# Softmax reciprocals spread over the keys by DMA through DRAM instead of by matmuls, with four score slots, in a cross-attention kernel

## The chip, the cores and the metric

The kernel runs on one core of one Trainium2 chip. The metric is the device time of one execution in microseconds (us). The kernel before takes 1735.91 us, the median of three runs (1733.51 to 1736.13).

## The reference

Cross-attention of 16 batches, 1024 query tokens each, with 64 context keys, 16 heads of 64 columns and a model width of 512; then a residual and a layer norm. Cut to what matters:

```python
qh = (q @ Wq + bq).reshape(Bn, Tq, H, DK)
kh = (k @ Wk + bk).reshape(Bn, Tk, H, DK)
vh = (v @ Wv + bv).reshape(Bn, Tk, H, DK)
attn = jnp.einsum('bqhd,bkhd->hbqk', qh, kh)
attn = attn * mask[None]
attn = attn - jnp.max(attn)
attn = jnp.exp(attn) * mask[None]
attn = attn / (jnp.sum(attn, axis=-1, keepdims=True) + 1e-15)
out = jnp.einsum('hbqk,bkhd->bqhd', attn, vh).reshape(Bn, Tq, H * DK)
out = out @ Wo + bo
x = out + residual
mu = jnp.mean(x, axis=-1, keepdims=True)
var = jnp.mean((x - mu) ** 2, axis=-1, keepdims=True)
return (x - mu) / jnp.sqrt(var + 1e-05) * gamma + beta
```

The maximum is taken over all scores of all batches, so no exponential can be formed before the last score is known. The sum that divides is one number for each token and head, and it divides that head's 64 keys.

## The kernel before

The kernel is written engine by engine: SP issues every DMA (one queue), and PE, ACT, DVE and POOL each have their own list of instructions, in the order in which the code lists them, with semaphores between them. Nothing reorders the work. There are two phases.

**Scores phase** (`scores_phase`, up to 917 us). Query and key weights are folded into one matrix for each batch, values and output weights into another, U. A *unit* is one batch's half of the tokens (512 of them); there are 32 units, four to a group (`UNITS`), eight groups. A unit's scores are a tile of 128 partitions (two heads of 64 keys) x 8 head pairs x 512 tokens, float32, 2 MB. Units 2 to 31 of the output phase's order are written to DRAM (`scores_d`); the last two that are made stay in SBUF in the two slots of `s32` and become units 0 and 1.

**Output phase** (`output_phase`, from 917 us on). In unit n:

- PE makes the unit's output: four token blocks t of 128, for each the eight head pairs p, and for each of these three float16 matmuls (L79 to L81, `add_product`): 96 matmuls with 512 columns. In between it does work for later units. `sums(n + 2)` (L792, before block t = 1, pair p = 7) adds the exponentials of unit n + 2 over each head's keys: 16 matmuls, as float32. `spread(n + 1, p)` (L804, eight places in the unit, table `spread_at`) copies the reciprocals of unit n + 1 from the few partitions where they stand to all 64 keys of each head, into a PSUM bank `ps_bc`. PE has float32 only in pieces here, so the reciprocal is first cut into three bfloat16 parts (`r_hi`, `r_mid`, rest).
- ACT rounds the scaled exponentials to float16 (`round_p`, L870), forms the exponentials of unit n + 2 in two halves in place (`exps`, L856), puts the bias into the output banks (`fill`, L875), cuts the reciprocals (`r_first`, `r_second`, L860, L864) and applies the norm (`norm`, L880).
- DVE multiplies exponentials and spread reciprocals (`scale_p`, L960, SBUF times PSUM into PSUM), takes the rounding rest (`split_p`, L964), inverts the sums (`invert`, L941 and L943), makes the second and third part of the reciprocals (L947, L954), adds the residual and takes the layer norm's statistics (`residual`, L975 to L980) and its shift (`shift_of`, L986).
- POOL computes 1 / sqrt(var + eps) (L1061, L1064) and applies gamma and beta (L1071, L1073).
- SP loads scores of unit n + 2 into the slot that unit n leaves (L722), the input x of unit n + 2 (L730), U of a batch in every second unit (L734), and stores the output of unit n - 1 (L740).

ACT's last two calls in a unit are `fill(n + 1, 3)` and `norm(n, 3)`. `norm(n, 3)` has to wait for PE's last block of unit n, then for DVE's statistics, POOL's `rstd` and DVE's shift, so it runs when PE is some us into unit n + 1. ACT's calls for unit n + 1 stand behind it.

Of the kernel before, what the change touches and what calls it, by code (L numbers as in the profile page):

```python
# [13 lines left out]
P = 128  # L14
# [8 lines left out]
TT = 512  # L23
# [18 lines left out]
COPIES = 3  # L42


def build(nc, xT, x, ctxT, maskT, wk, wqT, wv, wo, bk, bq, bv, bo, gamma, beta,
          sel_sum_d, sel_bc_d, part_d, out):

    scores_d = nc.dram_tensor("scores", (NU - UB, P, NP * TT), F32, kind="Internal").ap()
    u_d = nc.dram_tensor("u_halves", (B, P, NP * 2 * D), F16, kind="Internal").ap()

    with ExitStack() as ctx:
        def sb(name, shape, dt=F32, scope=ctx):
# [4 lines left out]
        sel_sum, sel_bc = sb("sel_sum", [P, NP // 2, 32]), sb("sel_bc", [P, NP, 2, P], BF16)  # L57
# [3 lines left out]
        scores_phase(nc, xT, ctxT, maskT, wk, wqT, wv, wo, bk, bq, bv, sel_bc_d, scores_d, u_d,  # L61
                     s32, sel_bc, score_max, least)
        output_phase(nc, x, scores_d, u_d, bo, gamma, beta, sel_sum_d, part_d, out,
                     s32, sel_sum, sel_bc, score_max, least, key_max, neg_max)
# [59 lines left out]
def scores_phase(nc, xT, ctxT, maskT, wk, wqT, wv, wo, bk, bq, bv, sel_bc_d, scores_d, u_d,  # L124
                 s32, sel_bc, score_max, least):

    with ExitStack() as ctx:
# [96 lines left out]
        def _(sp):  # L224
# [6 lines left out]
            def load_sel():  # L231
                sp.wait_ge(w_lo_done, 16)
                for i in range(2):
                    sp.dma_start(w32[:, i, :], sel_bc_d[i]).then_inc(w_loaded(16 + i)[0], 16)

# [43 lines left out]
            def group(g, first, last):  # L279
# [8 lines left out]
                for u in range(UNITS):  # L288
# [6 lines left out]
                    if first and u == 2:  # L295
                        load_sel()
# [115 lines left out]
        def _(act):  # L412
# [59 lines left out]
            def copy_sel(i):  # L472
                act.wait_ge(*w_loaded(16 + i))
                act.activation(sel_bc[:, 4 * i:4 * i + 4, :, :].rearrange("r p t k -> r (p t k)"),
                               w32[:, i, :], ACT.Copy)

            def scores_out(g, u, first, last):
# [11 lines left out]
                for p in range(NP):  # L489
# [16 lines left out]
                    if first and u == 2 and p in (3, 5):  # L506
                        copy_sel(p // 4)
# [149 lines left out]
def output_phase(nc, x, scores_d, u_d, bo, gamma, beta, sel_sum_d, part_d, out,  # L657
                 s32, sel_sum, sel_bc, score_max, least, key_max, neg_max):
# [3 lines left out]
    with ExitStack() as ctx:  # L662
# [13 lines left out]
        part = sb("part", [P, 2])  # L676
# [8 lines left out]
        r32, rest = ps_sum[:, HT:2 * HT], ps_sum[:, 0:HT]  # L685

# [448 lines left out]
```

## Time and profile before

| | |
|---|---|
| median of three runs | 1735.91 us (1733.51 to 1736.13) |
| profiled execution, its own time | 1737.56 us |
| its span, first to last instruction | 1735.8 us |
| PE busy | 1676.3 us, 97% |
| DVE / ACT / POOL busy | 1153.6 / 938.8 / 419.0 us |
| DMA | 315 MB, 181 GB/s over the span |
| scores phase / junction / output phase | 0 to 917 / 917 to 950 / 950 to 1736 us |

The span is one execution taken by the profiler; its own time lies 1.76 us over the span and 1.65 us over the median. Busy PE time counts overlapping matmuls once, so 97% says that PE rarely waits, not that it is at its peak. A matmul of 512 columns is shown with 380 ns, but the next one starts 216 ns after it.

### The profile page before, as it was taken

How to read it: one execution, taken by the hardware profiler on the slowest of the kernel's cores; microseconds unless marked ns; L12 is line 12 of the kernel's file. 1: busy time of each engine (PE TensorE's matmuls, PEld its weight loads, DVE VectorE, ACT ScalarE, POOL GpSimd, SP SyncE). 2: the span in 40 equal slices, each digit the busy share in tenths (PEclk: the TensorE clock that was granted, in tenths of full speed). 3: DMA queues.
4: the chain of work that ended last, by engine and by line, in shares of the span. 5: the costliest groups of instructions: out<-in, count | busy, mean ns of one | idle time of the engine just before them, and what ended most of it. 6: DMA issues, size and time to landing. Idle time of an engine off the chain costs nothing. (4 is left out here: it accounts for less than half of the span.)

```text
span 1735.8 us, 31156 instructions
## 1 busy us (share of the span) xinstructions
PE 1676.3 (97%) x11011; PEld 858.7 (49%) x11012; DVE 1153.6 (66%) x2346; ACT 938.8 (54%) x1413; POOL 419.0 (24%) x519
## 2 busy tenths in 40 slices
PE   4989999999999999999995999999999999999997
PEld 4545556455564655646542444444444444444443
DVE  7756555655556654565544877787787878787774
ACT  7745555455555555455544556555555656555542
POOL 0000000000000000000000455555555555555556
PEclk8999999999999999999996999999999999999999
DMA  6464344443544526445235356555654556555621
GB/s 231 146 230 141 146 182 163 178 167 121 205 159 161 187 91 235 137 168 196 74 146 209 139 230 242 217 206 205 242 209 186 194 233 242 217 201 210 242 104 67
DMA packets 81469, 315.01 MB, mean 181 GB/s; under 512 B 5392, under 2 KB 9616, under 8 KB 71696
## 3 DMA queue, kind: packets, MB, share of 16 engines
q1 hardware_dynamic: 81424, 314.41, 49.4%
q8 instruction: 28, 0.46, 0.1%
q14 instruction: 17, 0.14, 0.0%
HBM read 184.37 MB, written 130.02 MB: 181 GB/s over the span
## 5 line engine op out<-in xcount | busy, mean ns | idle before, releaser
L70 PE MATMUL ps_s<-x_hi,g_hi 128*128 128x512 f16 x1024 | 388.4, 379 | 7.0 <-ACT s L494 7.0
L79 PE MATMUL ps_o<-u,p_hi 128*128 128x512 f16 x1024 | 389.3, 380 | 0.0
L80 PE MATMUL ps_o<-u,p_hi 128*128 128x512 f16 x1024 | 388.9, 380 | 0.0
L81 PE MATMUL ps_o<-u,p_lo 128*128 128x512 f16 x1024 | 388.6, 380 | 0.0
L71 PE MATMUL ps_s<-x_lo,g_hi 128*128 128x512 f16 x1024 | 388.1, 379 | 0.0
L72 PE MATMUL ps_s<-x_hi,g_lo 128*128 128x512 f16 x1024 | 388.1, 379 | 0.0
L494 ACT ACTIVATE s<-ps_s,c_bias 128x512 f32<-128x512 f32 x256 | 175.8, 687 | 334.1 <-PE ps_s L72 330.2
L603 DVE TENSOR_TENSOR score_max<-score_max,tile_max 128x1 f32<-128x1 f32 x257 | 40.8, 159 | 339.2 <-ACT s L494 336.9
L870 ACT ACTIVATE p_hi<-ps_bc 128x512 f16<-128x512 f32 x256 | 149.4, 593 | 178.5 <-DVE ps_bc L960 176.6
L1051 POOL PARTITION_ALL_REDUCE key_max<-score_max x1 | 0.4, 377 | 922.8 <-issue 922.8
L1071 POOL TENSOR_TENSOR y<-y,gamma_b 128x512 f32<-128x512 f32 x128 | 162.7, 1271 | 192.7 <-ACT y L880 192.7
L960 DVE TENSOR_TENSOR ps_bc<-s,ps_bc 128x512 f32<-128x512 f32 x256 | 174.3, 692 | 19.4 <-PE ps_bc L804 15.8
L964 DVE TENSOR_TENSOR p_lo<-ps_bc,p_hi 128x512 f16<-128x512 f32 x256 | 175.4, 685 | 4.4 <-ACT p_hi L870 3.7
L613 DVE CUSTOM_DVE_ANT_0 s<-s,mask_add 128x512 f32<-128x512 f32 x256 | 176.6, 690 | 0.0
L880 ACT ACTIVATE y<-y,shift,rstd 128x512 f32<-128x512 f32 x128 | 104.0, 813 | 131.2 <-DVE shift L986 131.2
L1073 POOL TENSOR_TENSOR y<-y,beta_b 128x512 f32<-128x512 f32 x128 | 162.5, 1270 | 10.0
L70 PEld LDWEIGHTS ps_s<-x_hi,g_hi 128*128 128x128 f16 x1024 | 100.1, 98 | 130.8 <-issue 10.3
L81 PEld LDWEIGHTS ps_o<-u,p_lo 128*128 128x128 f16 x1024 | 100.3, 98 | 121.5 <-issue 1.1
L72 PEld LDWEIGHTS ps_s<-x_hi,g_lo 128*128 128x128 f16 x1024 | 100.2, 98 | 120.9
L71 PEld LDWEIGHTS ps_s<-x_lo,g_hi 128*128 128x128 f16 x1024 | 100.2, 98 | 112.0
L79 PEld LDWEIGHTS ps_o<-u,p_hi 128*128 128x128 f16 x1024 | 100.3, 98 | 104.4 <-issue 14.0
L80 PEld LDWEIGHTS ps_o<-u,p_hi 128*128 128x128 f16 x1024 | 100.4, 98 | 91.1 <-issue 0.6
(85 smaller groups left out, 2423.0 us busy)
## 6 DMA issues: line engine op xcount, KB each, us to landing
scores<-s SPq DMA_DIRECT2D x30, 2048.0 KB, 7.6
s<-scores SPq DMA_DIRECT2D x30, 2048.0 KB, 7.7
x<-xT_in SPq DMA_DIRECT2D x32, 1024.0 KB, 9.7
u_halves<-u_out SPq DMA_DIRECT2D x64, 512.0 KB, 2.9
u<-u_halves SPq DMA_DIRECT2D x16, 2048.0 KB, 11.8
y<-x_in SPq DMA_DIRECT2D x32, 1024.0 KB, 10.0
out<-y SPq DMA_DIRECT2D x31, 1024.0 KB, 4.3
mask<-maskT_in SPq DMA_DIRECT2D x32, 256.0 KB, 10.3
```

The source lines that it names most:

```text
L70: pe.matmul(out, lhs_hi, rhs_hi, start=first, stop=False)
L71: pe.matmul(out, lhs_hi, rhs_lo, start=False, stop=False)
L72: return pe.matmul(out, lhs_lo, rhs_hi, start=False, stop=last)
L79: pe.matmul(out, lhs_hi, rhs_hi, start=False, stop=False, skip_group_check=True)
L80: pe.matmul(out, lhs_hi, rhs_lo, start=False, stop=False, skip_group_check=True)
L81: return pe.matmul(out, lhs_lo, rhs_hi, start=False, stop=False, skip_group_check=True)
L494: act.activation(s32[:, u % 2, p, :], ps_s[p % SBANKS][:, :], ACT.Identity, bias=c_bias[:, k:k + 1], scale=1 / (G_SCALE * X_SCALE)).then_i ...
L613: dve.tensor_tensor_reduce(s32[:, u % 2, p, :], s32[:, u % 2, p, :], mask_add[:, j, t0:t0 + TT], 1.0, MASKED, ALU.add, ALU.max, tile_max[: ...
L960: dve.tensor_tensor(spread, s32[:, s, p, :], spread, ALU.mult).then_inc(p_scaled, 1)
L964: dve.tensor_tensor(p_lo[:, s, p, :], ps_bc[p % RBANKS][:, :], p_hi[:, s, p, :], ALU.subtract)\
L1071: pool.tensor_tensor(y, y, gamma_b[:, :], ALU.mult).then_inc(scaled, 1)
L1073: pool.tensor_tensor(y, y, beta_b[:, :], ALU.add).then_inc(shifted, 1)
```

## The change

The reciprocals are no longer multiplied out by PE. DVE writes them into SBUF (`r32`, [128, 2, 256], already scaled), SP stores them to a small DRAM tensor `r_d` with four DMAs of 8 partitions x 256 numbers (`store_r`), waits until all four have landed, and reads them back with four DMAs, each into 64 partitions x 4 pairs x 512 tokens, in which every one of a head's 64 partitions gets the same row (`spread_r`, 512 KB a DMA, 2 MB a unit). The three bfloat16 parts, the selector matrix `sel_bc` and its load are gone. `scale_p` multiplies two SBUF tiles and writes PSUM. There are four score slots (two in `s32`, two in `s_more`), and SP loads scores three units ahead instead of two. ACT's two `exps` move to the start of a unit's list, PE's `sums` from (1, 7) to (1, 0), DVE's `invert` from behind `split(3)` to behind the first `residual`.

The diff, cut to its core:

```diff
+    r_d = nc.dram_tensor("reciprocals", (2, NP, 2, TT), F32, kind="Internal").ap()
...
-        den = sb("den", [P, HT])
-        r_hi, r_mid, r_all = sb("r_hi", [P, HT], BF16), sb("r_mid", [P, HT], BF16), sb("r_all", [P, 2, HT], BF16)
+        s_more = sb("s_more", [P, 2, NP, TT])
+        den, r32 = sb("den", [P, 2, HT]), sb("r32", [P, 2, HT])
+        r_bc = sb("r_bc", [P, 2, NP, TT])
...
-        spread_at = {(0, 2): 0, (0, 5): 1, (1, 0): 2, (1, 3): 3, (1, 6): 4, (2, 1): 5, (2, 4): 6, (2, 7): 7}
-        sums_at = (1, 7)
+        sums_at = (1, 0)
+
+        def scores_of(u):
+
+            return (s32 if u % UNITS < 2 else s_more)[:, u % 2, :, :]
...
             def load_scores(n, u):
-                sp.wait_ge(p_scaled, (n - 1) * NP)
+                if not isinstance(n, int) or n >= UNITS:
+                    sp.wait_ge(p_scaled, (n - UNITS + 1) * NP)
...
+            def store_r(n, s):
+
+                sp.wait_ge(r_done, n + 1)
+                for q in range(4):
+                    th, a = q // 2, q % 2
+                    sp.dma_start(r_d[s, 4 * a:4 * a + 4, :, th * HT:(th + 1) * HT].rearrange("p h t -> (p h) t"),
+                                 r32[32 * q:32 * q + NP, s, :]).then_inc(r_stored, 16)
+
+            def spread_r(n, s):
+
+                sp.wait_ge(r_stored, 64 * n + 64)
+                for k in range(2):
+                    for h in range(2):
+                        row = r_d[s, 4 * k:4 * k + 4, h:h + 1, :].rearrange("p a t -> a p t")
+                        sp.dma_start(r_bc[rows_of(h), s, 4 * k:4 * k + 4, :], row.to_broadcast([NK, 4, TT]))\
+                          .then_inc(bc_in[s][k], 16)
...
             sp.dma_start(sel_sum[:, :, :], sel_sum_d).then_inc(sum_in, 16)
-            sp.dma_start(part[:, :], part_d).then_inc(sum_in, 16)
+            load_scores(2, 2)
+            load_scores(3, 3)
             load_u(0, B - 1)
...
+            for n in range(2):
+                store_r(n, n)
+                spread_r(n, n)
...
+                    n = g * UNITS + u
+                    if not (first and u == 0):
+                        store_y(g, u - 1)
                     if not (last and u >= UNITS - 2):
-                        load_scores(g * UNITS + u + 2, u)
+                        store_r(n + 2, u % 2)
+                        spread_r(n + 2, u % 2)
+                    if not (first and u == 0) and not (last and u >= UNITS - 3):
+                        load_scores(n + 3, u + 3)
+                    if not (last and u >= UNITS - 2):
                         load_x(g, u + 2)
...
+            pe.wait_ge(u_in[0], 16)
             for o in ps_o:
-                mm = pe.matmul(o[:, :], sel_bc[:, 0, 0, :], sel_bc[:, 0:2, :, :].rearrange("r p t k -> r (p t k)"),
-                               start=True, stop=True)
+                mm = pe.matmul(o[:, :], u2[:, 0, 0, 0, 0:P], u2[:, 0, 0, 0, :], start=True, stop=True)
             mm.then_inc(o_written, 1)
...
-                    halves(0, 1)
                     if more2:
-                        exps(n + 2, u, 0)
-                    halves(2)
+                        exps(n + 2, u + 2, 0)
+                    halves(0)
                     if more2:
-                        exps(n + 2, u, 1)
-                    halves(3)
+                        exps(n + 2, u + 2, 1)
+                    halves(1, 2, 3)
...
+            def scale_p(n, u, p):
+                s = u % 2
+                if p % 4 == 0:
+                    dve.wait_ge(bc_in[s][p // 4], 16 * n - 16 * s + 32)
...
+                dve.tensor_tensor(ps_p[p % RBANKS][:, :], scores_of(u)[:, p, :], r_bc[:, s, p, :], ALU.mult)\
+                   .then_inc(p_scaled, 1)
```

How the instructions stand on SP, first before, in unit 2 of group 0 (out names the tile written; `y` is the residual and output tile):

```order
L722 DMA s<-scores 128x4096 [waits p_scaled]
L730 DMA y<-x_in 128x4x512 [waits y_stored0]
L734 DMA u<-u_halves 128x8192 [waits o_summed]
L740 DMA out<-y 128x4x512 [waits shifted]
L722 DMA s<-scores 128x4096 [waits p_scaled]
```

and in the changed kernel, for the same unit:

```order
L744 DMA out<-y 128x4x512 [waits shifted]
L718 DMA reciprocals<-r 8x256 [waits r_done]
L718 DMA reciprocals<-r 8x256 x3
L727 DMA r_bc<-reciprocals 64x4x512 [waits r_stored]
L727 DMA r_bc<-reciprocals 64x4x512 x3
L709 DMA s<-scores 128x4096 [waits p_scaled]
L734 DMA y<-x_in 128x4x512 [waits y_stored0]
L738 DMA u<-u_halves 128x8192 [waits o_summed]
```

The scores' load, which stood first, now stands behind eight new DMAs and the two waits in front of them.

ACT's list at the change of units, first before (the last norm of a unit, then the next unit, in the last group):

```order
L880 ACTIVATE y<-y,shift,rstd 128x512 [waits shift_done]
L870 ACTIVATE p_hi<-ps_bc 128x512 [waits p_scaled,o_summed]
L870 ACTIVATE p_hi<-ps_bc 128x512 [waits p_scaled]
L856 ACTIVATE s<-s,neg_max 128x2x1024 [waits s_in1]
L870 ACTIVATE p_hi<-ps_bc 128x512 [waits p_scaled]
L856 ACTIVATE s<-s,neg_max 128x2x1024 [waits s_in1]
```

and in the changed kernel:

```order
L871 ACTIVATE y<-y,shift,rstd 128x512 [waits shift_done]
L855 ACTIVATE s_more<-s_more,neg_max 128x2x1024 [waits s_in3]
L861 ACTIVATE p_hi<-ps_p 128x512 [waits p_scaled,o_summed]
L855 ACTIVATE s_more<-s_more,neg_max 128x2x1024 [waits s_in3]
```

The exponentials stand two roundings earlier, but still behind the previous unit's last norm.

PE's list around the sums in the last group (`ps_sum` holds the sums), first before, in the second token block:

```order
L804 MATMUL ps_bc<-r_all,sel_bc 128x256 [waits p_lo_done]
L804 MATMUL ps_bc<-r_all,sel_bc 128x256
L79 MATMUL ps_o<-u,p_hi 128x512
L80 MATMUL ps_o<-u,p_hi 128x512
L81 MATMUL ps_o<-u,p_lo 128x512
L792 MATMUL ps_sum<-s,sel_sum 32x256 [waits exp_done,r_all_done]
L792 MATMUL ps_sum<-s,sel_sum 32x256 x7
L792 MATMUL ps_sum<-s,sel_sum 32x256 [waits exp_done]
```

and in the changed kernel, where the first token block ends:

```order
L78 MATMUL ps_o<-u,p_hi 128x512 [waits p_lo_done]
L79 MATMUL ps_o<-u,p_hi 128x512
L80 MATMUL ps_o<-u,p_lo 128x512
L806 MATMUL ps_sum<-s_more,sel_sum 32x256 [waits exp_done,den_done,bo_filled]
L806 MATMUL ps_sum<-s_more,sel_sum 32x256 x7
L806 MATMUL ps_sum<-s_more,sel_sum 32x256 [waits exp_done]
L806 MATMUL ps_sum<-s_more,sel_sum 32x256 x7
L78 MATMUL ps_o<-u,p_hi 128x512
```

Before, 15 triples of the unit and five of its eight `ps_bc` pairs stood ahead of the sums. Now eight triples do, and the `ps_bc` pairs are gone.

## Rows read from the trace of the kernel before

**Rows 1.** Windows of the output phase: us, busy of PE, PEld, DVE, ACT, POOL, PEclk, DMA, GB/s.

```profile
950.50:1683.50 733.00, 733.00 (x4313) 353.96 (x4312) 582.07 (x1076) 411.75 (x598) 386.48 (x474) 1.00 0.55 210
...
1268.11:1292.54 24.43, 24.43 (x145) 11.81 (x144) 19.45 (x36) 13.72 (x20) 13.06 (x16) 1.00 0.45 170
```

**Rows 2.** Chain that ended last, in order of time: start us, us, what.

```profile
1254.64 1.86 PE ps_sum L792 x32
1279.07 1.86 PE ps_sum L792 x32
```

**Rows 3.** Timeline of PE, unit 13: start us, us, engine, line, operation.

```profile
1268.11 0.38 PE L79 MATMUL ps_o<-u,p_hi 128*128 128x512 f16 x1
...
1278.04 0.38 PE L804 MATMUL ps_bc<-r_all,sel_bc 128*128 128x256 bf16 x2
...
1279.00 1.93 PE L792 MATMUL ps_sum<-s,sel_sum 128*32 128x256 f32 x32
1280.87 0.39 PE L79 MATMUL ps_o<-u,p_hi 128*128 128x512 f16 x1
...
1292.54 0.38 PE L79 MATMUL ps_o<-u,p_hi 128*128 128x512 f16 x1
```

**Rows 4.** Timeline of ACT, from a unit's last norm through the next unit's exponentials.

```profile
1271.80 0.81 ACT L880 ACTIVATE y<-y,shift,rstd 128x512 f32<-128x512 f32 x1 [2.17 <-DVE shift L986]
...
1273.50 2.00 ACT L856 ACTIVATE s<-s,neg_max 128x2048 f32<-128x2048 f32 x1
1275.39 0.59 ACT L870 ACTIVATE p_hi<-ps_bc 128x512 f16<-128x512 f32 x1
1275.87 2.00 ACT L856 ACTIVATE s<-s,neg_max 128x2048 f32<-128x2048 f32 x1
```

**Rows 5.** Timeline of DVE: an inversion; a unit's last shift and the next unit's first scales.

```profile
1256.57 0.42 DVE L941 TENSOR_SCALAR den<-ps_sum 128x256 f32<-128x256 f32 x1 [1.25 <-PE ps_sum L792]
1257.03 1.76 DVE L943 RECIPROCAL ps_sum<-den 128x256 f32<-128x256 f32 x1
...
1271.55 0.21 DVE L986 TENSOR_SCALAR shift<-mean_var,rstd 128x1 f32<-128x1 f32 x1 [1.57 <-POOL rstd L1064]
1271.68 1.29 DVE L960 TENSOR_TENSOR ps_bc<-s,ps_bc 128x512 f32<-128x512 f32 x2
```

**Rows 6.** Timeline of POOL across the same change of units.

```profile
1269.48 1.27 POOL L1073 TENSOR_TENSOR y<-y,beta_b 128x512 f32<-128x512 f32 x1
...
1272.69 1.27 POOL L1071 TENSOR_TENSOR y<-y,gamma_b 128x512 f32<-128x512 f32 x1 [1.18 <-ACT y L880]
```

**Rows 7.** Timeline of SP, the store of the previous unit's output.

```profile
1275.59 0.40 SPq L740 DMA_DIRECT2D out<-y  x1
```

**Rows 8.** DMA issues: operation, count, KB each, median us from issue to landing.

```profile
s<-scores SPq DMA_DIRECT2D x30, 2048.0 KB, 7.7
...
y<-x_in SPq DMA_DIRECT2D x32, 1024.0 KB, 10.0
...
out<-y SPq DMA_DIRECT2D x4, 256.0 KB, 2.0
```

**Rows 9.** DMA rates in 40 slices of 104 to 114 us; the low ones are mask loads.

```profile
GB/s 369 377 369 377 377 385 385 369 426 426 434 295 213 254 213 246 221 197 172 172 172 172 262 385 434 418 410 426 393 377 361 442 377 442 393 426 442 393 442 393
```

**Rows 10.** DMA rates in 40 slices of 924 to 934 us; gamma, beta, bo repeated over partitions.

```profile
GB/s 328 459 524 393 352 238 262 361 352 402 385 279 123 131 115 147 74 172 197 238 295 254 262 311 369 401 385 410 434 410 410 401 401 393 418 401 418 401 352 328
```

**Rows 11.** PE in windows around the junction: us, PE busy, PEclk, DMA share, GB/s.

```profile
925.96:929.74 3.78, 3.72 (x32) 0.53 1.01 230
...
947.60:950.08 2.48, 0.01 (x2) 0.99 0.95 405
950.08:953.04 2.96, 2.96 (x9) 0.50 1.04 381
```

**Rows 12.** Timeline: the first exponentials, and DVE's first work after PE's last matmul.

```profile
923.81 3.89 ACT L856 ACTIVATE s<-s,neg_max 128x2048 f32<-128x2048 f32 x2 [7.59 <-DVE neg_max L1031]
...
1726.92 0.69 DVE L975 SCALAR_TENSOR_TENSOR y<-ps_o,y 128x512 f32<-128x512 f32 x1 [2.36 <-PE ps_o L81]
```

More of the change, by code:

```diff
@@ L684, in output_phase @@
         ps_sum = bank("ps_sum")
-        r32, rest = ps_sum[:, HT:2 * HT], ps_sum[:, 0:HT]
-        ps_bc = [bank(f"ps_bc{i}") for i in range(RBANKS)]
+        ps_p = [bank(f"ps_p{i}") for i in range(RBANKS)]
         ps_o = [bank(f"ps_o{i}") for i in range(OBANKS)]
@@ L792, in sums @@
                         mm = pe.matmul(ps_sum[32 * q:32 * q + 32, 0:HT], sel_sum[:, i, :],
-                                       s32[:, s, p, th * HT:(th + 1) * HT],
+                                       scores_of(u)[:, p, th * HT:(th + 1) * HT],
                                        start=(i == 0), stop=(i == 3), skip_group_check=True)
                 mm.then_inc(e_summed, 1)
-            def spread(n, s, p):
-                if p == 0:
-                    pe.wait_ge(r_all_done, n + 1)
-                pe.wait_ge(p_lo_done, n * NP + (p + 1 if p >= RBANKS else (2, 3, 1)[p]))
-                for th in range(2):
-                    mm = pe.matmul(ps_bc[p % RBANKS][:, th * HT:(th + 1) * HT], sel_bc[:, p, th, :], r_all[:, s, :],
-                                   start=True, stop=True)
-                mm.then_inc(r_spread, 1)
             def unit(g, u, last):
                 n, s, b = g * UNITS + u, u % 2, u // UB
-                more, more2 = not (last and u == UNITS - 1), not (last and u >= UNITS - 2)
+                more2 = not (last and u >= UNITS - 2)
                 if u % UB == 0:
@@ L817, in unit @@
                     for p in range(NP):
[L818 to L819 removed]
                         if more2 and (t, p) == sums_at:
[L821 removed]
+                            sums(n + 2, u + 2)
                         if t == 0:
[L823 removed]
+                            pe.wait_ge(p_lo_done, n * NP + p + 1)
                         cols = slice(t * P, (t + 1) * P)
@@ L918, in _ @@
             exps(1, 1, 1)
-            r_first(0)
-            r_second(0)
             act.wait_ge(affine_in, 48)
@@ L926, in _ @@
                     fill(0, p // 2)
-            r_first(1)
-            r_second(1)
             with act.Fori(0, NG - 1) as g:
@@ L992, in group @@
                     more, more2 = not (last and u == UNITS - 1), not (last and u >= UNITS - 2)
-                    scale = lambda p: scale_p(n, s, p) if more else None
+                    scale = lambda p: scale_p(n, u + 1, p) if more else None
                     split = lambda p: split_p(n, s, p) if more else None
@@ L1122 @@
         "bo": a["bo"], "gamma": a["gamma"], "beta": a["beta"],
[L1123 removed]
+        "sel_sum": sel_sum,
     }
```

141 lines of the change are left out of this document (40 added, 101 removed).

## The prediction

> **What bounds the kernel now.** I read the windows first: from 950.5 to 1683.5 us PE is busy for all 733 us at full clock (level 2.4 GHz), while DVE has 19.45 us of work in a unit, ACT 13.7, POOL 13.1, and the DMA engines are half used [rows 1]. So the output phase is PE's own time. The chain of waits says the same: it runs through PE only, and the sums of one unit start 24.43 us after those of the unit before [rows 2]. A unit (here 13, from 1268.11 to 1292.54) is thus 24.43 us: 96 matmuls 0.216 us apart, 20.75; sums 1.87 (1279.00 to 1280.87); and what is left, 1.81, is the eight pairs of `ps_bc` matmuls [rows 3]. The change takes away those 1.81 us, 31 times, at most 56 us. The rest of this text asks what the unit waits for instead.
>
> **What hides at no cost.** `r_first`, `r_second`, the second and third part on DVE and the selector's load go; they lay beside PE's work. The scores phase is otherwise as it was.
>
> **Sums and exponentials.** Call U the start of a unit on PE. PE now wants the sums of unit n + 2 after eight triples, at U + 5.2. The exponentials stand behind the previous unit's last norm on ACT. That norm starts at U + 3.7 (1271.80), after DVE's shift (1271.55), which waited for POOL, which first finished the affine begun at 1269.48 [rows 4 to 6]. The change moves nothing of this. So the first exponential starts at E = U + 4.4 at the earliest. The first half ends 2.0 us later, one rounding lies between, and the second half ends at E + 4.4 (1273.50 to 1277.87) [rows 4]. The first half of the sums can end at E + 3.0, the second at E + 5.4, which is U + 9.8. PE wanted to be through at U + 7.1 and stalls 2.7 us. With 24 triples behind it (15.55) a unit is at least 25.4 us. If POOL were free sooner, E would be U + 3.7 and the unit 24.7. Either way, what the spreads gave back is gone here alone. Before, this stall was not there, because PE asked at U + 10.9 for halves that ended at U + 9.8.
>
> **The ring of waits through the DMA queue.** SP issues in the order: output of n - 1, four stores of the reciprocals of n + 2, wait until landed, four spreads, scores of n + 3, x, U. The scores of n + 3 are wanted by the exponentials at the start of the next unit, E'. So E' hangs on E:
>
> - exponentials, both halves: 4.4 [rows 4];
> - second half of the sums: 0.95 at full clock; 1.9 after a stall, since after 2.5 us without work PE's clock is at 0.50 (1.2 GHz) for the next 3 us, and the sums at 926 took 3.78 us instead of 1.86 [rows 2, 11]. Taken: 1.9;
> - DVE adds and inverts: 2.2 (1256.57 to 1258.79) and 0.1 to get there [rows 5]. `r_done` at E + 8.6;
> - four stores. An issue holds SP 0.4 us [rows 7], and a small transfer, 256 KB, lands 2.0 us after it [rows 8]: 0.1 + 1.2 + 2.0 = 3.3. At E + 11.9. SP stands still for that, with the scores, x and U of the unit queued behind;
> - spreads: 0.9 from issue to first data (an estimate: 7.7 us for 2 MB less 6.0 of transfer at 350 GB/s and 0.8 of landing) [rows 8], then 2 MB in 64-partition DMAs that repeat one row over the partitions. No row has this. Nearest in width are the mask loads, 64 partitions each: eleven slices between 172 and 295 GB/s, mean 212, with 370 to 430 on both sides [rows 9]; 2.10 MB at 212 is 9.9 us. Nearest in source are the three loads that repeat one row over 128 partitions: 0.79 MB pass in about 3.5 us, 230 GB/s, six slices of it at 127 [rows 10]. From below: 400 GB/s as the neighbours have, 5.2 us. From above: 127, 16.5 us. I take 10.5, by the masks with a little for the source;
> - scores, 2.10 MB at the 400 GB/s of a filled queue [rows 9]: 5.2, landing 0.8 [rows 8].
>
> Sum 4.4 + 1.9 + 2.3 + 3.3 + 0.9 + 10.5 + 5.2 + 0.8 = 29.3; 29.4 with rounding. This is more than the 25.4 that PE and ACT need, so the ring sets the period, and PE stands still some 5 us in each unit. After the stall up to 3 us of matmuls run at half clock [rows 11], 1.5 us lost, but they are covered: U' = E + 6.3 + 1.5 + 15.55 = E + 23.4, and with 4.4 that is E + 27.8, below 29.4. x and U (2.6 and 5.2 us) of an even unit end at about E' + 7, the store of the output (issued at U' + 7.5 [rows 7], 2.6 us) behind them at E' + 9.6, before the reciprocals' stores should land at E' + 11.9; so they don't lengthen it.
>
> The Trainium skill, SBUF — State Buffer, section "Door 1: The DMA port swizzle", says that 64 partitions in a row reach only 8 of 16 ports, half of 435 GB/s. By that the spreads would take 9.6 us instead of 10.5 and the forecast would be 24 us lower; the masks' mean of 212 agrees with it.
>
> DVE loses 0.96 us of work in a unit. `scale_p` reads two SBUF tiles; I keep its 0.6 us start to start (1271.68, 1.29 for two) [rows 5].
>
> **Junction.** Before, unit 1 starts at 975.0 (1268.11 less 12 x 24.43). Now SP first issues 4 MB of scores, U, three repeated rows and 2 MB of x from 918 us on. PE waits for U before its first sums: 919 + 3 x 5.2 = 935. `r_done` of unit 0 is at about 941 (before 932: exponentials from 923.81 [rows 12], sums and inversion). Its stores land at 946 behind x, half its spread at 953. DVE and ACT need 1.2 us for each pair, the second four wait for the other half at 958.4: PE has the eighth pair at 963.5. The spread of unit 1 is issued only after the first (SP waits for its stores), its first half lands at 965.6. ACT's second exponential for unit 2 stands behind the first rounding of unit 1, so it ends at 969, the sums at 970, and unit 1 starts at 970 + 15.6 = 986, 11 us later. Its E is 990; it still finds its scores loaded. The next E, with the first load behind a spread, is 990 + 8.6 + 3.3 + 0.9 + 10.5 + 5.2 + 0.8 = 1019.
>
> **The sum.** E of unit 2 at 1019, unit 29 (the last with sums) 27 x 29.4 later, 1813; unit 30 starts 23.4 later, 1836; units 30 and 31 have neither sums nor spreads, 41.5; from PE's last matmul to the end 8.9 (1726.9 to 1735.8) [rows 12]. Span 1887, and with the 1.8 us outside the span **1889 us**, against 1737.6 for the profiled execution, which is 1.65 above the median. With the spreads between 7.8 and 13 us the ring is 26.7 to 32, the time 1820 to 1960.
>
> **Rivals.**
> - *The DMAs are fast enough; only the sums wait* (0.17). With the spreads at 400 GB/s the ring is 24.1 and the unit 24.7 to 25.4. Unit 2's E is then about 1016; 27 units, 21.0, 41.5, 8.9 and 1.8 give 1756 to 1775. For it: the queue moves 2 MB in 5.2 us when 128 partitions are written. Against: the masks.
> - *The repeated rows are a hot spot* (0.12). All engines read the same few rows; at the six slices' 127 GB/s the spread is 16.5 us, the ring 35.4, the time 1889 + 27 x 6 = 2051. For it: those slices. Against: they last 1.5 us of 3.5.
> - *Faster* (0.06). The one mechanism: ACT's exponentials and the loads come before PE asks. It would need E at U + 1.7 or sooner, so that both halves are summed by U + 7.1, and a ring under 22.6 us. A unit is then 22.6: 986 + 29 x 22.6 + 41.5 + 8.9 + 1.8 = 1694. For it: PE is the only busy engine. Against: the norm at U + 3.7.
> - *DVE and POOL get in each other's way* (0.03). POOL's affine reads SBUF for 1.27 us twice a block [rows 6], and `scale_p` now has both inputs there. If each of eight scales waited for one such instruction, DVE had 18.5 + 10.2 = 28.7 us a unit: alone 1737.6 + 11 + 29 x 4.3 = 1873, and nothing where the ring is 29.4. On average a scale would meet POOL in 0.42 of cases and wait half of it: 2 us, no time. The Trainium skill, SBUF — State Buffer, has this rule (a VectorE instruction with two SBUF inputs and a GpSimd instruction that reads SBUF block each other); the trace before has no such pair.
>
> **How the numbers follow.** Forecast 0.62, the rivals 0.17, 0.12, 0.06, 0.03. The likeliest's time is 1889. The range goes down to 1755 to take in the sums' stall alone and up to 1990 for spreads of up to 14 us; faster and most of the hot spot stay outside, 0.18. A measurement tells 0.2%, 3.5 us, from no change. Faster 0.06, same 0.02 (the stall's low edge with a shorter junction), slower 0.92.
>
> **What would show it.** In the profile of the changed kernel: a period of 29.4 us between sums; PE idle some 5 us before the sums, released by ACT's exponentials, and these by the scores' DMA; PEclk under 1.00 in most slices of the output phase; DMA at 200 to 220 GB/s while `r_bc` is written, SP's longest wait for the stored reciprocals or `r_done`. It is wrong if the exponentials follow the norm at once (first rival), or if sums aren't waited for.

## The result, and the profile after

The changed kernel takes 1873.09 us (median of 4 runs, 1869.21 to 1875.29), the kernel before 1736.02 in the same session (4 runs). The ratio is 1.0789, 95% interval 1.0767 to 1.0811: slower by 137 us. The forecast was 1889, with a range from 1755 to 1990. The profiled execution of the changed kernel took 1872.35 us, its span is 1870.5.

The windows of the changed kernel's output phase, all of it from unit 2 to unit 27, then one period, then the 2.5 us behind its sums, answer to [rows 1] (us, busy of PE, PEld, DVE, ACT, POOL, PEclk, DMA, GB/s):

```profile
1019.00:1760.00 741.00, 641.78 (x3293) 272.06 (x3294) 528.39 (x875) 342.91 (x464) 357.69 (x408) 0.91 0.79 254
...
1417.80:1446.60 28.80, 25.32 (x133) 10.86 (x132) 21.85 (x35) 13.40 (x19) 14.43 (x17) 0.94 0.71 220
...
1429.50:1432.00 2.50, 2.50 (x12) 0.99 (x9) 2.38 (x4) 0.00 (x0) 0.74 (x2) 0.66 0.00 0
```

PE was busy for 733 of 733 us; now it stands still for 99 of 741, 3.5 in the period shown, and in the 2.5 us after that its mean clock is 0.66 of full (0.50, the 1.2 GHz level, until 1431.0). The DMA engines went from 0.55 to 0.79 of their time. The chain that ended last ran through PE alone [rows 2]. Now it runs through the queue, in order of time (start, us, what):

```profile
1459.59 1.76 DVE r L927
...
1462.38 1.29 DMA reciprocals<-r
1463.69 0.59 SPq L727
...
1466.51 14.18 DMA s<-scores
...
1483.20 1.41 ACT s L855
```

This is the ring of the prediction: inversion, stores, spreads, the scores' load behind them, exponentials, the next inversion (1488.36). One link is another than the prediction's: from the exponentials the chain goes through ACT's rounding and DVE's `split` and `residual` to the inversion, and not through PE's sums, which end 0.9 us before DVE comes to it. One turn of it on SP's timeline (`reciprocals<-r` are the four stores, `r_bc` the four spreads; `xN` runs together are one row):

```profile
1432.69 1.31 SPq L718 DMA_DIRECT2D reciprocals<-r  x4
1435.01 2.57 SPq L727 DMA_DIRECT2D r_bc<-reciprocals  x4
1437.85 0.61 SPq L709 DMA_DIRECT2D s_more<-scores  x1
```

From the spreads at 1059.00 to these at 1435.01 there are 13 periods, 28.92 us each. ACT and PE in the same period, first ACT's norm and exponentials, answering to [rows 4]:

```profile
1421.57 0.81 ACT L871 ACTIVATE y<-y,shift,rstd 128x512 f32<-128x512 f32 x1 [2.24 <-DVE shift L963]
1423.26 2.00 ACT L855 ACTIVATE s_more<-s_more,neg_max 128x2048 f32<-128x2048 f32 x1 [0.88 <-DMA s_more<-scores]
1425.17 0.58 ACT L861 ACTIVATE p_hi<-ps_p 128x512 f16<-128x512 f32 x1
1425.65 1.99 ACT L855 ACTIVATE s_more<-s_more,neg_max 128x2048 f32<-128x2048 f32 x1
```

then PE's sums (here in the last unit that has them), answering to [rows 3]:

```profile
1798.24 1.07 PE L806 MATMUL ps_sum<-s_more,sel_sum 128*32 128x256 f32 x16 [2.60 <-ACT s_more L855]
1800.52 1.93 PE L806 MATMUL ps_sum<-s_more,sel_sum 128*32 128x256 f32 x16 [1.21 <-ACT s_more L855]
1802.39 0.61 PE L78 MATMUL ps_o<-u,p_hi 128*128 128x512 f16 x1
```

PE waits before each half of the sums for ACT. The second half takes 1.93 us instead of the first one's 1.07, and the matmuls behind it 0.61 instead of 0.38: the granted clock is 0.50 (1.2 GHz) from 1800.5 to 1802.4, after two idle stretches of 2.6 and 1.2 us. ACT waits only 0.88 us for the scores, so the ring is just a little longer than what the engines would need by themselves.

DVE, answering to [rows 5], for the inversion:

```profile
1428.16 0.69 DVE L941 TENSOR_TENSOR p_lo<-ps_p,p_hi 128x512 f16<-128x512 f32 x1 [1.08 <-ACT p_hi L861]
1428.77 0.68 DVE L952 SCALAR_TENSOR_TENSOR y<-ps_o,y 128x512 f32<-128x512 f32 x1
...
1430.25 0.18 DVE L957 BATCH_NORM_AGGREGATE mean_var<-stats 128x2 f32<-128x6 f32 x1
1430.45 0.42 DVE L924 TENSOR_SCALAR den<-ps_sum 128x256 f32<-128x256 f32 x1
1430.91 1.75 DVE L927 RECIPROCAL r<-den 128x256 f32<-128x256 f32 x1
```

The DMA rates in 40 slices of 0.5 us from 1434 to 1454, so the spreads of this period and the scores behind them:

```profile
GB/s 23 10 0 0 41 176 344 217 180 270 254 229 201 205 213 246 221 209 205 213 246 217 205 483 143 492 492 393 295 426 492 524 459 143 377 410 406 414 487 483
```

From slice 5 to slice 23 (1436.2 to 1445.5) the rate is mostly 201 to 254 GB/s: 2.1 MB of spreads in 9.3 us, 226 GB/s on average. Behind them the scores move mostly at 377 to 524.

### The profile page after: what moved, and what is told of

Its sections match the earlier page's. It is cut to its first block, busy times and chain, and to the rows that moved or that the text cites. A ratio compares the mean times of both kernels' runs of the same rounds, so it can differ in the third digit from the quotient of the medians.

```text
span 1870.5 us, 30251 instructions
## 1 busy us (share of the span) xinstructions
PE 1684.5 (90%) x10500; PEld 818.7 (44%) x10500; DVE 1183.3 (63%) x2282; ACT 923.1 (49%) x1347; POOL 448.3 (24%) x519
## 4 chain that ended last, share of the span: by engine, by line
DMA 25%; DVE 6%; issue 5%; SPq 5%; PE 5%; ACT 4%; POOL 1%; DVEq 0%; ACTq 0%; POOLq 0%
DMA s<-scores 11%; DMA s_more<-scores 11%; SPq L727 3%; DVE r L927 2%; DMA reciprocals<-r 2%; ACT p_hi L861 2%; PE ps_o L78 1%; PE ps_o L79 1%; PE ps_o L80 1%; ACT s_more L855 1%; SPq L718 1%; DVE stats L955 1%; DVE y L952 1%; ACT s L855 1%; DMA u<-u_halves 1%
## 5 line engine op out<-in xcount | busy, mean ns | idle before, releaser
L78 PE MATMUL ps_o<-u,p_hi 128*128 128x512 f16 x1024 | 402.5, 393 | 13.4 <-ACT ps_o L866 12.3
L79 PE MATMUL ps_o<-u,p_hi 128*128 128x512 f16 x1024 | 400.6, 391 | 0.0
L80 PE MATMUL ps_o<-u,p_lo 128*128 128x512 f16 x1024 | 397.9, 389 | 0.0
L861 ACT ACTIVATE p_hi<-ps_p 128x512 f16<-128x512 f32 x256 | 147.5, 589 | 307.1 <-DVE ps_p L936 307.0
L941 DVE TENSOR_TENSOR p_lo<-ps_p,p_hi 128x512 f16<-128x512 f32 x256 | 175.1, 684 | 116.0 <-ACT p_hi L861 115.8
L1039 POOL TENSOR_TENSOR y<-y,gamma_b 128x512 f32<-128x512 f32 x128 | 167.7, 1310 | 233.2 <-ACT y L871 233.2
L1041 POOL TENSOR_TENSOR y<-y,beta_b 128x512 f32<-128x512 f32 x128 | 174.6, 1364 | 10.0
L78 PEld LDWEIGHTS ps_o<-u,p_hi 128*128 128x128 f16 x1024 | 102.6, 100 | 163.3 <-issue 35.6
L79 PEld LDWEIGHTS ps_o<-u,p_hi 128*128 128x128 f16 x1024 | 102.5, 100 | 122.5 <-issue 10.6
L936 DVE TENSOR_TENSOR ps_p<-s,r_bc 128x512 f32<-128x512 f32 x128 | 113.9, 901 | 12.7 <-DMA r_bc<-reciprocals 10.1
```

The lines of the kernel that those rows point to most:

```text
L78: pe.matmul(out, lhs_hi, rhs_hi, start=False, stop=False, skip_group_check=True)
L79: pe.matmul(out, lhs_hi, rhs_lo, start=False, stop=False, skip_group_check=True)
L80: return pe.matmul(out, lhs_lo, rhs_hi, start=False, stop=False, skip_group_check=True)
L861: act.activation(p_hi[:, s, p, :], ps_p[p % RBANKS][:, :], ACT.Copy).then_inc(p_hi_done, 1)
L941: dve.tensor_tensor(p_lo[:, s, p, :], ps_p[p % RBANKS][:, :], p_hi[:, s, p, :], ALU.subtract)\
L1039: pool.tensor_tensor(y, y, gamma_b[:, :], ALU.mult).then_inc(scaled, 1)
```

## The experiments

Theories, as the expectations name them: the **ring** through SyncE's queue sets the unit; the **sums** come too early in the unit; the **queue** is simply full; **VectorE's list** (with GpSimd) holds the unit. "Period" below is the mean distance of the spreads' issues between 1050 and 1600 us.

**1. Sums at (1, 7) and the inversion behind `split(3)` again.**

```diff
-        sums_at = (1, 0)
+        sums_at = (1, 7)
...
                     split(3)
+                    if more2:
+                        invert(n + 1, 1 - s)
```

> The changed kernel with PE's sums back at (1, 7) and DVE's inversion back behind split(3). Theory A (the ring: exponentials, sums, inversion, stores, spreads, then the scores' load behind them): the period stays 28 to 29 us, since the load of the scores still stands behind the spreads; 1855 to 1875 us. Theory B (the sums are asked for too early, PE's stall sets the unit): the stall goes, the unit is 22.6 to 24.5 us, 1700 to 1750 us. Theory C (the DMA queue is full: 7 MB a unit, 2 of them at half rate): unchanged, 1873 us.

1937.81 us (1935.21 to 1938.56), ratio 1.1158 (1.1139 to 1.1176): 65 us slower than the changed kernel. All three theories missed. The period is 31.4 us (1064.45 to 1597.68, 17 periods), and ACT waits for the scores:

```profile
1425.83 2.00 ACT L855 ACTIVATE s<-s,neg_max 128x2048 f32<-128x2048 f32 x1 [4.62 <-DMA s<-scores]
```

The inversion is itself in the ring. Behind `split(3)` it began at 1435.61, 9.8 us after the exponentials (7.2 in the changed kernel), though PE had ended the sums at 1432.1; so every spread is late, and with it the scores behind. The two edits were not tried one by one, but the trace puts the 2.5 us a unit on the inversion. The theory of early sums is refuted as the cause of the time; the ring stands, but I had left the inversion's place out of it when I wrote 1855 to 1875.

**2. The scores' load ahead of the stores and spreads.**

```diff
                     n = g * UNITS + u
+                    if not (first and u == 0) and not (last and u >= UNITS - 3):
+                        load_scores(n + 3, u + 3)
                     if not (first and u == 0):
                         store_y(g, u - 1)
...
-                    if not (first and u == 0) and not (last and u >= UNITS - 3):
-                        load_scores(n + 3, u + 3)
```

> The changed kernel with SP issuing the scores of unit n + 3 first in the unit, ahead of the output store, the reciprocals' stores and the spreads. Theory A: the ring is cut; what remains is the norm, then two exponentials, then the sums: 25.4 us a unit if PE keeps its clock through the two short stalls, 27.9 if it does not, 1780 to 1850 us. Theory B: the same 1780 to 1850. Theory C: the bytes are the same, so no change, 1865 to 1875 us.

1833.08 us (1831.75 to 1834.03), ratio 1.0560 (1.0542 to 1.0578), 40 us faster than the changed kernel. The exponentials now follow the norm at once:

```profile
1426.75 0.81 ACT L871 ACTIVATE y<-y,shift,rstd 128x512 f32<-128x512 f32 x1 [3.26 <-DVE shift L963]
1427.47 1.99 ACT L855 ACTIVATE s_more<-s_more,neg_max 128x2048 f32<-128x2048 f32 x1
```

The period is 27.5 us (1055.09 to 1576.78, 19 periods). So the ring was what set 28.9, and the queue was not full: the same bytes now take 40 us less. But cutting the ring gives back only these 40 of the 137 us. What is left is a second loop, and it is not PE's: between 1100 and 1370 us no piece of the chain is on PE. It goes through the layer norm and DVE's list, some lines of a unit:

```profile
1284.91 1.27 POOL y L1039
1286.26 1.26 POOL y L1041
...
1289.30 0.46 ACT s_more L855
...
1293.56 0.59 ACT p_hi L861
...
1294.79 0.69 DVE y L952
```

POOL's gamma and beta hold its next `rstd`, that holds the last norm, the exponentials stand behind the norm, the roundings behind the exponentials, and DVE's `split` and `residual` behind the roundings. PE's stall for the sums follows from this loop, and its slow clock costs next to nothing. Of two periods, from exponential to exponential, one has slow matmuls in it and the other none (PEclk 0.94 and 1.00), and they are equally long:

```profile
1289.30:1316.76 27.46, 24.47 (x130) 10.46 (x128) 21.98 (x36) 13.28 (x19) 14.21 (x16) 0.94 0.75 231
1400.02:1427.47 27.45, 23.81 (x132) 10.31 (x130) 22.23 (x36) 13.15 (x19) 14.21 (x16) 1.00 0.71 217
```

PE is in the chain in single periods only; the one with ten slow matmuls (from 1378) took 28.4.

**3. Both.**

> Both edits, e1 and e2. Theory A: neither the ring nor the early sums hold PE; the unit is PE's own 22.6 us or what the DMA queue needs for its bytes (5.2 MB at 400 GB/s and 2.1 MB at 215: 23 us), 1695 to 1730 us, below the kernel before. Theory B: about the same as e1, 1700 to 1750. Theory C: no change, 1865 to 1875 us.

1801.65 us (1800.33 to 1802.54), ratio 1.0376 (1.0359 to 1.0393). A miss by over 70 us, but with the ring cut the late sums and inversion now help by 31, where alone they cost 65. The period is 26.4 us. DVE waits 2.77 us for POOL's rstd, then 1.95 and 1.08 for ACT's roundings, which stand behind the two exponentials:

```profile
1409.39 0.21 DVE L963 TENSOR_SCALAR shift<-mean_var,rstd 128x1 f32<-128x1 f32 x1 [2.77 <-POOL rstd L1032]
1412.86 0.69 DVE L941 TENSOR_TENSOR p_lo<-ps_p,p_hi 128x512 f16<-128x512 f32 x1 [1.95 <-ACT p_hi L861]
1415.23 0.69 DVE L941 TENSOR_TENSOR p_lo<-ps_p,p_hi 128x512 f16<-128x512 f32 x1 [1.08 <-ACT p_hi L861]
```

**4 to 6. What makes the spreads slow: their width or their repeated rows.** Three versions of the changed kernel with other sources and widths for `r_bc`, of the same 2 MB: in the first, four DMAs of 128 partitions that repeat rows of x; in the second, 128 partitions with rows of x of their own; in the third, 64 partitions as in the change, with rows of their own. The factors are then rows of x instead of the reciprocals. The first one's edit:

```diff
-                        row = r_d[s, 4 * k:4 * k + 4, h:h + 1, :].rearrange("p a t -> a p t")
-                        sp.dma_start(r_bc[rows_of(h), s, 4 * k:4 * k + 4, :], row.to_broadcast([NK, 4, TT]))\
+                        i = 4 * k + 2 * h
+                        row = x[s:s + 1, i:i + 2, :]
+                        sp.dma_start(r_bc[:, s, i:i + 2, :], row.to_broadcast([P, 2, TT]))\
```

> The changed kernel, with the four spreads replaced by four loads of the same 512 KB that repeat two rows of x over all 128 partitions (the factors are then not the reciprocals). If the width of 64 partitions makes the 215 GB/s: near 400 GB/s, 2 MB in 5.3 us, time 1780 to 1850 us. If the repeated row makes it: 215 GB/s or less, 1870 us.

> The same with each partition reading rows of x of its own, 128 partitions: 400 GB/s under either reading, 2 MB in 5.3 us, time 1780 to 1850 us.

> The same with 64 partitions a load and rows of its own for each. If the width makes the 215 GB/s: 215 GB/s again, 1870 us. If the repeated row makes it: near 400 GB/s, 1780 to 1850 us.

| spreads | time, single run | landing of one from 1400 to 1500, median us | period |
|---|---|---|---|
| as changed: 64 partitions, repeated | 1872.35 | 7.7 | 28.9 |
| 128 partitions, repeated | 1830.49 | 5.6 | 27.6 |
| 128 partitions, own rows | 1827.17 | 4.8 | 27.5 |
| 64 partitions, own rows | 1863.25 | 7.4 | 28.5 |

The rates in slices of 0.25 us, first 128 partitions with own rows (1434 to 1444), then 64 with own rows (1428 to 1438):

```profile
GB/s 0 0 0 0 0 123 131 172 311 393 434 410 402 410 410 410 401 336 246 352 410 401 385 344 393 410 410 467 729 549 197 852 66 590 393 393 655 197 524 393
```

```profile
GB/s 21 0 0 0 0 0 0 33 74 221 401 401 262 205 197 246 172 229 205 319 254 188 213 213 188 254 164 229 295 238 254 197 205 238 172 238 188 254 287 229
```

The width decides: some 410 GB/s with 128 partitions and some 215 with 64. The hot spot, a rival of the prediction, is refuted: repeated rows cost 3 us of the kernel's time at full width and 9 at half, by single runs, where the four runs of the changed kernel alone lie 6 us apart. With fast spreads the kernel is still some 90 us slower than before: the period stops at 27.5, at the loop of experiment 2 (POOL's gamma and beta have 18 to 19% of the chain in experiments 2, 4 and 5). The Trainium skill, SBUF — State Buffer, "Door 1: The DMA port swizzle", gives half the rate for 64 partitions in a row; the traces agree (some 215 against some 410 GB/s).

**7. Two queues: the halves for partitions 64 to 127 from ACT's queue.**

```diff
+            def spread_act(n, s):
+                act.wait_ge(r_stored, 64 * n + 64)
+                for k in range(2):
+                    spread_half(act, s, k, 1)
...
-                    halves(4, 5)
+                    halves(4)
+                    if more2:
+                        spread_act(n + 2, u % 2)
+                    halves(5)
```

> The changed kernel, in which ACT's queue issues the two spreads to partitions 64 to 127 and SP the two to partitions 0 to 63, so that both halves of the partitions can be written at once. If the 215 GB/s of the spreads is a limit of writing 64 partitions at a time: the 2 MB land in 5 to 6 us instead of 9.5, the ring falls to about 24.5, and the norm and exponentials' 25.4 to 27.9 us a unit are left, 1780 to 1850 us. If it is a limit of reading the same rows over and over: still 9.5 us, 1870 us.

1861.77 us (1857.78 to 1864.64), ratio 1.0717 (1.0697 to 1.0736), 11 us under the changed kernel. Both queues issue at the same time (1432.15 and 1432.16), one half for each side of the partitions, and together they still move 190 to 300 GB/s (1431 to 1441, slices of 0.25 us):

```profile
GB/s 16 33 33 0 0 0 0 0 0 0 172 270 303 188 221 238 246 197 287 295 246 254 238 221 238 197 197 213 188 229 262 229 221 229 213 213 246 377 549 574
```

So the two halves don't run side by side: the time is near the 1870 us expected for repeated rows, but experiments 4 to 6 rule that reason out. Over 6.75 us from the first data on, two queues move 232 GB/s on average and the changed kernel's one queue 227 (1436.5 to 1443.25). The Trainium skill, SBUF — State Buffer, "Can I just issue two DMAs to hit both halves?", says so too: it has a gain of 6%, here it is 2%. Why the chip does it is not shown by these traces. SP also issues two spreads less, 1.3 us in each turn; whether the 11 us come from there was not separated.

**8. Experiment 3 with ACT's exponentials behind `halves(0, 1)` and `halves(2)`, as before the change.**

> e3 (scores' load first, sums at (1, 7)) with ACT's two exponentials back behind the first two and the third rounding, as in the kernel before. Theory D (what holds e3 at 26.5 us a unit is DVE's list: it stands still for 1.95 and 1.08 us behind roundings that ACT has put behind its exponentials): some 2.5 us a unit come back, 24 us, 1725 to 1740 us. Theory C (the DMA queue needs 26 us for its bytes): no change, 1795 to 1805 us.

1762.51 us (1758.43 to 1763.97), ratio 1.0142 (1.0121 to 1.0164): 39 us faster than experiment 3, and still 22 above what I expected. The period is no longer even. SP's timeline:

```profile
1398.43 1.31 SPq L718 DMA_DIRECT2D reciprocals<-r  x4
1406.13 2.57 SPq L727 DMA_DIRECT2D r_bc<-reciprocals  x4
...
1425.85 1.30 SPq L718 DMA_DIRECT2D reciprocals<-r  x4
1429.36 2.57 SPq L727 DMA_DIRECT2D r_bc<-reciprocals  x4
```

The four stores of 8 KB, which needed 2.3 us from issue until the spreads could go, take 3.5 in one unit and 7.7 in the next: they stand behind the loads of x, U and scores. The spreads come 23.2 and 27.3 us apart in turn, a pair in 50.6 on average over ten; the long one is the unit whose stores stand behind U's 2 MB.

**9. Experiment 8 without gamma and beta on POOL** (they are replaced by two operations on one column, so the output lacks them).

> e8 without POOL's two affine instructions a block: gamma and beta are left out of the output, and two instructions on one column stand in their place. If DVE's scale_p, with both inputs in SBUF, and POOL's reads of SBUF hold each other up: scale_p's mean falls from 0.84 to 0.90 us to the 0.69 us of the kernel before in all units, and the unit gets 1 to 2 us shorter than e8's, 1670 to 1710 us. If scale_p is longer for another reason (its operands, the DMA writes): its mean stays at 0.84 or more, and the time falls by no more than what the wait for rstd gives, under 1 us a unit.

1757.19 us (1751.31 to 1762.17), ratio 1.0126 (1.0103 to 1.0149). That is far from the 1670 to 1710 expected, and its runs overlap with those of experiment 8, so no gain in time is shown. DVE's scales, by line, in experiment 8 and here (columns: count, busy us, mean ns, idle before):

```profile
L937 DVE TENSOR_TENSOR ps_p<-s,r_bc 128x512 f32<-128x512 f32 x128 | 114.2, 903 | 15.9 <-DMA r_bc<-reciprocals 15.8
```

```profile
L938 DVE TENSOR_TENSOR ps_p<-s,r_bc 128x512 f32<-128x512 f32 x128 | 86.5, 687 | 42.4 <-DMA r_bc<-reciprocals 42.4
```

The scales fall from some 0.90 us to 0.687, so POOL's two operations do hold them up, by 1.7 us in a unit of eight scales. But what DVE gains it now waits for `r_bc`, and the chain has long pieces of the queue in it:

```profile
1344.39 8.58 DMA reciprocals<-r
...
1353.63 7.00 DMA r_bc<-reciprocals
```

**10. Experiment 8 with another order of SP's first DMAs:** U first, then scores 2 and x 0, and x 1 and scores 3 behind the two first spreads.

> e8 with SP's first DMAs of the output phase in another order: U first, scores of unit 2 and x of unit 0 ahead of the stores and spreads of units 0 and 1, scores of unit 3 and x of unit 1 behind them. PE's first sums then don't wait for U behind 4 MB of scores: unit 1 starts 8 to 14 us earlier than in the changed kernel, and the time is 8 to 14 us under e8's. If the junction is bound by the exponentials and spreads alone, within 3 us of e8's.

1755.39 us (1753.36 to 1758.81), ratio 1.0102 (1.0085 to 1.0119): 7 us under experiment 8, just short of the 8 to 14 expected; the pair of units is as long as there (50.7 against 50.6 us), so the gain lies in the junction. This is the fastest order found.

**11. Experiment 10 with the stores issued from ACT's queue.**

```diff
                     halves(4, 5)
+                    if more2:
+                        store_r(n + 2, u % 2)
```

> The version before this one (1755.4 us) with the reciprocals' four stores issued from ScalarE's queue, behind halves(4, 5), with one semaphore per slot, so that they do not stand behind the loads of x, U and scores in SyncE's queue. There the stores were issued at 1442.67 and the spreads at 1449.01, 6.3 us later; the store itself needs about 2.3 us where nothing is ahead of it. Theory queue (small stores wait behind bulk in their own queue, and that closes the ring): the spreads follow the stores by 2.3 to 3.5 us, VectorE no longer waits for r_bc, the unit loses up to 1 us: 1725 to 1745 us. Theory VectorE and GpSimd (the unit of 24.2 us is held by shift, which waits 1.57 and 2.77 us for GpSimd's rstd, and by scales that take 0.90 instead of 0.69 us): the spreads come earlier, the time stays: 1750 to 1757 us.

1761.64 us (1760.81 to 1762.58), ratio 1.0144 (1.0129 to 1.0160): 6 us slower, and both theories missed. The stores no longer stand behind loads in their own queue, but from the last issue to the spreads it still takes 4.3 us, where an idle queue took 1.3. And they are issued 2.2 us later than `r_done` (1443.6), since ACT comes to them behind a rounding. ACT's queue in the chain:

```profile
1445.82 0.27 ACTq L863
...
1446.81 4.27 DMA reciprocals<-r
...
1451.10 0.59 SPq L719
```

**12. Experiment 11 with POOL's inverse deviation of tile t + 1 ahead of gamma and beta of tile t.**

```diff
+                    inv_std(g, u, 0)
                     for t in range(TB):
-                        inv_std(g, u, t)
+                        if t + 1 < TB:
+                            inv_std(g, u, t + 1)
                         affine(g, u, t)
```

> The version with the stores on ScalarE's queue, and on GpSimd the inverse deviation of tile t + 1 ahead of gamma and beta of tile t. Theory VectorE and GpSimd: the last shift of a unit, which waited 2.77 us for rstd, and the one that waited 1.57 us, wait under 0.6 us; the unit falls from 24.2 us towards the 22.6 us of its 96 matmuls and the sums (20.75 + 1.9): 31 times 1 to 1.6 us, 1700 to 1725 us, under the kernel before (1736). Theory queue alone: no change against the version with the stores moved, within 3 us. A third way: gamma and beta of a tile now wait for the mean of the next one, so y is stored later and the load of x behind it; with four slots of y that has a unit of slack, so nothing is lost.

1766.10 us (1765.84 to 1766.68), ratio 1.0169 (1.0155 to 1.0183): a miss, 4 us slower again. The last shift's wait fell from 2.8 us, in most units of experiment 11, to 1.56, but gamma and beta now lie beside the next scales, whose mean rose from 0.79 to 1.10 us (below, two of them take 3.23):

```profile
1434.85 0.21 DVE L966 TENSOR_SCALAR shift<-mean_var,rstd 128x1 f32<-128x1 f32 x1 [1.56 <-POOL rstd L1035]
1435.05 3.23 DVE L939 TENSOR_TENSOR ps_p<-s,r_bc 128x512 f32<-128x512 f32 x2
```

**What the versions have in common.** Windows from 1100 to 1600 us give the DMA engines' share; the distance of spreads gives a pair of units (U is loaded once for a pair; for the kernel before, 2 x 24.43). The row of experiment 10, as an example:

```profile
1100.00:1600.00 500.00, 464.83 (x2534) 203.30 (x2533) 404.32 (x671) 262.28 (x356) 287.19 (x317) 0.97 0.91 292
```

| | DMA share | pair of units, us | DMA busy in a pair, us |
|---|---|---|---|
| before | 0.57 | 48.9 | 27.9 |
| changed | 0.80 | 57.8 | 46.3 |
| 128 partitions, repeated (4) | 0.69 | 55.2 | 38.1 |
| exponentials after (8) | 0.91 | 50.6 | 46.1 |
| without gamma and beta (9) | 0.92 | 50.2 | 46.2 |
| first DMAs reordered (10) | 0.91 | 50.7 | 46.1 |
| stores from ACT (11) | 0.90 | 51.2 | 46.1 |
| POOL ahead (12) | 0.90 | 51.5 | 46.3 |

Orders change the pair, not the last column. The spreads add 18.4 us to it, 9.2 a unit, for which the change takes 1.8 us a unit from PE. A pair of PE's work without spreads is 45.2 us (2 x 22.6). So as changed, the DMA engines have as much to do as PE, and in the best orders they are busy for 91% of the time. The rest shows in the rates of experiment 10 from 1436 to 1456, in slices of 0.5 us:

```profile
GB/s 492 524 492 459 393 262 492 524 492 426 360 328 492 492 492 393 229 492 287 397 418 414 406 267 8 0 0 0 29 156 332 213 209 254 238 238 201 205 205 254
```

Up to 1448 the queue works off U, x and scores, the stores (issued at 1442.67) among the last of them. Then nothing moves for some 2.3 us, while SP learns that they have landed and issues the spreads (1449.01). Twice in a pair that is 4.6 of 50.7 us, the 9%. That the full queue sets these last 20 us is argued from these rates, not shown: in experiment 10 stores and spreads have only 22% of the chain from 1100 to 1600 us, the rest lies mostly on DVE, ACT, POOL and PE or between their instructions, and no version moved fewer bytes in this order. Experiment 9 speaks for it, where faster scales brought no time. With spreads at full width (experiment 4) 8 us of the queue's time in a pair would be free again. That was not tried together with the better order, since a DMA that takes one row for partitions 0 to 63 and another for 64 to 127 has not been built here, so whether the idea can beat the kernel before stays open. None of the twelve does.

## Why the prediction was right, point by point

The ring held, in the place and the order given but for one link, and the time was 17 us off (1889 against 1872.35 for the profiled execution). What would set the unit without the ring was right in size and wrong in its reason, and there the forecast was lucky. By its steps:

- **PE's share of the gain.** 1.81 us a unit are gone from PE, and nothing of it reached the time, as said: 24.4 became 28.9.
- **Sums.** The unit's first matmul was at about 1417.8, the norm at U + 3.8 (1421.57), as said. E came at U + 5.5 and not U + 4.4, since ACT waited 0.9 us for the scores, which the ring implies. Both halves ended 4.4 after E (1423.26 to 1427.64), as said. The second half of the sums took some 1.9 in most units, as said; in those at 1225.55 and 1485.14 the clock had not fallen and it took 1.07. It made no odds, since the sums are not in the chain.
- **The bound without the ring.** It was put at 27.8, from PE's stall, its slow clock and 4.4 to the next exponential; with the ring cut it is 27.5. The number is luck: the loop that sets it runs through the norm, POOL, the exponentials and DVE's list, and has the same length where PE's clock didn't fall (experiment 2).
- **`r_done`.** Put at E + 8.6, was E + 9.4 (1432.66). I gave DVE 0.1 us to get to the inversion. It took 0.9: the change puts it behind the first `residual`, and that stood behind a `split` that waited 1.08 us for ACT's rounding.
- **Stores.** Put at 3.3, were 2.3 (1432.69 to 1435.01): the 8 KB land 1.3 us after the last issue, where I had taken the 2.0 of the 256 KB stores.
- **Spreads and scores.** 0.9 + 10.5 + 5.2 + 0.8 = 17.4 from the first spread's issue to the scores' landing; was 16.9 (1435.01 to 1451.92). The spread itself, the term with the widest bounds, took 9.3 where I said 10.5: the masks' 212 GB/s was right, and the "little for the source" I added to it was wrong, as experiments 4 to 6 show.
- **The ring**: 4.4 + 1.9 + 0.9 + 2.2 + 2.3 + 16.9 makes 28.6 for this turn, against 28.9 on average and 29.4 predicted. (1.9 + 0.9 is the sums and DVE's delay by the prediction's terms; by the chain the same 2.8 us are ACT's rounding and DVE's `split` and `residual`.) Over 27 periods 0.54 us are 14.6 of the 17 us.
- **Junction and end.** The first E was put at 990 and came at 987.14, the next at 1019 and came at 1016.99, the last at 1813 and came at 1796.10: (1796.10 - 1016.99) / 27 = 28.86 a period. From there to the end 74.4 us, predicted 73.8 (23.4 + 41.5 + 8.9). The other 2 us of the error are in the junction.

```profile
987.14 1.99 ACT L855 ACTIVATE s_more<-s_more,neg_max 128x2048 f32<-128x2048 f32 x1
...
1016.99 2.00 ACT L855 ACTIVATE s<-s,neg_max 128x2048 f32<-128x2048 f32 x1 [2.31 <-DMA s<-scores]
```

- **Signs.** Sums released by ACT and exponentials by the scores' DMA, DMA at 200 to 250 GB/s while `r_bc` is written, PEclk under 1.00: all seen. "PE idle some 5 us" was too much: 3.5 in the period shown, 3.9 on average.

Of the rivals, the one where only the sums wait gave 1756 to 1775 with fast spreads, and experiments 4 and 5 took 1827 to 1830. Its unit of 24.7 to 25.4 us left out the loop of experiment 2: the moved exponentials hold up ACT's roundings, and these DVE, which no part of the prediction counted. The hot spot is refuted. DVE and POOL do get in each other's way, 1.7 us a unit where I had said 2 on average. It did nothing to the forecast, as said, but I gave it too little weight for what comes after: POOL is in the chain of experiments 2, 4 and 5, and the longer scales return in 8 to 12.

What the prediction did not see at all is the last table: it treated the spreads as a piece of a chain, never as 9 us of all DMA engines in a unit. My expectations for experiments 3, 8, 9, 11 and 12 were too low each time. In 3 it was the loop through ACT's exponentials and roundings, and moving the exponentials back (experiment 8) gave 39 us; from 8 on, cutting one wait after the other seems only to have led to the full queue.

## What to carry to other kernels

When work is moved from a busy engine to DMA, work out two sums: the ring (what must land before the next issue, everything queued behind it included), and the DMA engines' own time per unit, with the rate that the destination's width gives. Here 1.8 us of PE were paid with 9.2 us of the queue. An order that helps in one state can hurt in another: a late inversion and late sums cost 65 us while the inversion closed the ring and gained 31 once the scores' load was ahead of it. Before a wait of the bottleneck is called the cause, see whether the chain runs through it: here PE stalled and slowed down, and another loop kept the time. Put loads with nothing to wait for ahead of those that wait in the same queue, and expect small latency-critical transfers to take several times longer behind bulk ones.

## What the runs showed of the hardware that I had not expected

- Two queues, one for partitions 0 to 63 and one for 64 to 127, move 232 GB/s together, hardly more than one over the same length of time (227), while DMAs over 128 partitions move some 410 (experiment 5).
- Four stores of 8 KB: from the last one's issue until SP goes on, 1.3 us with nothing else under way, 8.6 us in the row shown and up to 9.0 behind bulk loads in their own queue (experiment 9), and still 4.3 us from another queue beside bulk loads (experiment 11).
- A DVE multiplication of two SBUF tiles takes 0.69 us alone and up to 1.73 beside POOL's operations on SBUF. POOL is held too. DVE and POOL at the same time in the changed kernel:

```profile
1411.93 1.73 DVE L936 TENSOR_TENSOR ps_p<-s,r_bc 128x512 f32<-128x512 f32 x1
```

```profile
1411.83 1.27 POOL L1039 TENSOR_TENSOR y<-y,gamma_b 128x512 f32<-128x512 f32 x1 [1.27 <-ACT y L871]
1413.18 1.60 POOL L1041 TENSOR_TENSOR y<-y,beta_b 128x512 f32<-128x512 f32 x1
```

POOL's gamma began 0.1 us before and ended at 1413.10; the multiplication ended at 1413.66, 0.56 us later, as if it had started only then. POOL's beta, begun while DVE was at work, took 1.60 instead of 1.27 us. The Trainium skill, SBUF — State Buffer, "Who interferes with whom", has this rule for a VectorE instruction with two SBUF inputs and a GpSimd instruction that reads SBUF; experiment 9 agrees, with 0.687 us for every scale once POOL no longer works on SBUF tiles of that size.
